# A delta-rule stage of a vision tower: the decay mask moved into spare rows of a product, the inverse rows reordered, the output product cut in two

## What is computed

```python
q = silu(x @ Wq);  k = l2norm(silu(x @ Wk));  v = silu(x @ Wv)
log_f = log_sigmoid(x @ Wf);  gamma = -sigmoid(x @ Wgamma)
gk = log_f[..., None]
a = k * gamma[..., None] * exp(gk)
def step(S, inp):                      # over the 38 tokens of an image
    Sp = S * exp(gkt)[..., None]
    u = einsum('bhk,bhkv->bhv', at, Sp) + vt
    S = Sp + einsum('bhk,bhv->bhkv', kt, u)
    o = einsum('bhk,bhkv->bhv', qt, S)
out = out * sigmoid(x @ Wg1 @ Wg2)     # then a layer norm and @ Wo
```

## Time and profile before

| | |
|---|---|
| Median of 3 executions | 1996.59 us (1990.41 to 1997.77) |
| The profiled execution: its time | 1989.77 us |
| Its span, first to last instruction | 1988.0 us |
| Mean granted TensorE clock | 0.857 of 2.4 GHz |
| Busy: PE, DVE, ACT, POOL | 1708.2, 1108.5, 656.6, 314.5 us |
| The 11 delta stages | 1303.05 to 1819.19 us of the span |
| A stage with all four parts (3 to 7) | 57.8 to 61.7 us |

### The profile page before, as it was taken

How to read it: one execution, slowest core, us unless ns; L and a number is a source line. 1 busy time by engine, 2 the same in 40 slices (tenths; PEclk the granted TensorE clock), 3 DMA queues, 4 the chain that set the end, 5 groups by cost and what they waited for, 6 DMA issues and landing times. The chain is left out here.

```text
span 1988.0 us, 51796 instructions
## 1 busy us (share of the span) xinstructions
PE 1708.2 (86%) x22689; PEld 1517.3 (76%) x22689; DVE 1108.5 (56%) x2379; ACT 656.6 (33%) x1347; POOL 314.5 (16%) x284
## 2 busy tenths in 40 slices
PE   4677786799999999999999999876888888757589
PEld 4466675579988999989999999745877777756468
DVE  3655555674545555455555465566445555543885
ACT  3334534433322233232223232163333333223142
POOL 0232232520000000000000000052322223200530
PEclk9888988899999999999999999877666656655579
DMA  4100000100100000000101000100000000001001
GB/s 135 60 2 1 0 0 1 67 22 1 43 1 22 22 22 22 22 22 1 44 1 43 1 1 1 36 1 2 4 4 4 3 4 4 4 4 48 1 11 41
DMA packets 10070, 36.01 MB, mean 18 GB/s; under 512 B 3056, under 2 KB 6152, under 8 KB 7304
## 3 DMA queue, kind: packets, MB, share of 16 engines
q1 hardware_dynamic: 9864, 32.96, 4.8%
HBM read 30.47 MB, written 2.49 MB: 17 GB/s over the span
## 5 line engine op out<-in xcount | busy, mean ns | idle before, releaser
L1042 ACT ACTIVATE hidden<-bank,moe_b 128x512 f32<-128x512 f32 (+1 forms) x320 | 213.3, 668 | 537.1 <-PE bank L934 524.5
L951 PE MATMUL bank<-moe_w2h,hidden_hi 128*128 128x256 f32 x1216 | 345.7, 284 | 0.0
L951 PE MATMUL bank<-moe_w2l,hidden_hi 128*128 128x256 f32 x1216 | 344.0, 283 | 0.0
L951 PE MATMUL bank<-moe_w2h,hidden_lo 128*128 128x256 f32 x1216 | 343.9, 283 | 0.0
L934 PE MATMUL bank<-x_hi,moe_w1h 128*128 128x512 f32 (+1 forms) x640 | 243.8, 381 | 2.9 <-ACT hidden L1042 2.8
L934 PE MATMUL bank<-x_lo,moe_w1h 128*128 128x512 f32 (+1 forms) x640 | 242.5, 379 | 0.0
L934 PE MATMUL bank<-x_hi,moe_w1l 128*128 128x512 f32 (+1 forms) x640 | 242.0, 378 | 0.0
L951 PEld LDWEIGHTS bank<-moe_w2h,hidden_hi 128*128 128x128 f32 x1216 | 233.1, 192 | 6.0 <-DVE residual L1076 4.3
L1076 DVE SCALAR_TENSOR_TENSOR residual<-bank,gates,residual 128x256 f32<-128x256 f32 x152 | 73.4, 484 | 290.4 <-PE bank L951 290.4
L951 PEld LDWEIGHTS bank<-moe_w2l,hidden_hi 128*128 128x128 f32 x1216 | 233.2, 192 | 1.2
L951 PEld LDWEIGHTS bank<-moe_w2h,hidden_lo 128*128 128x128 f32 x1216 | 233.2, 192 | 0.0
(11 more groups left out here) (287 smaller groups left out, 3357.3 us busy)
## 6 DMA issues: line engine op xcount, KB each, us to landing
moe_w<-in_moe_w SPq DMA_DIRECT2D x16, 1024.0 KB, 4.8
patches<-in_patches SPq DMA_DIRECT2D x8, 864.0 KB, 4.6
out<-residual SPq DMA_DIRECT2D x19, 128.0 KB, 1.7
ffn_w<-in_ffn_w SPq DMA_DIRECT2D x2, 1024.0 KB, 6.4
att_w<-in_att_w SPq DMA_DIRECT2D x1, 1536.0 KB, 5.9
delta_w<-in_delta_w SPq DMA_DIRECT2D x1, 1280.0 KB
tok_w<-in_tok_w SPq DMA_DIRECT2D x1, 768.0 KB, 4.1
delta_wvf<-in_delta_wvf SPq DMA_DIRECT2D x1, 272.0 KB
```

The lines of the kernel that those rows point to most:

```text
L951: mm = nc.tensor.matmul(bank[4 + n % 3][:, 0:D], left, right, start=(i == 0), stop=(i == len(passes) - 1))
L1042: nc.scalar.activation(H[:, i % 4, 0:n], bank[i % 4][:, 0:n], ACT.Relu, bias=b1[:, x, f:f + 1]).then_inc(acted, 1)
```

## The change

- The mask product L1506 goes, and with it `past`. Instead the free 13 rows of each group of 32 carry it: `here` has 0/1 values there, scaled by 2^30, and `after` has -1 there where it had 0, so that the two remaining products give a large negative sum where the mask was. For this ln2 loads more pieces (8 of `here` now from two sources, and 8 of `free_row`), and DVE has more small operations in stage 0.
- DVE's inverse rows go ahead: 6 to 12 before bounded(0), 13 between bounded(0) and bounded(1), 14 and 15 before the low parts, 16 before weigh(0), 17 before unit_key(0), 18 before weigh(4).
- `output` becomes output(0) (images 0 to 3, banks 2 and 3) and output(1) (banks 0 and 1), in the order key_norm(0), output(0), key_norm(1), output(1). output(0) waits for solution(0) alone. The copies follow in the same two parts, as many and as large as before.
- inverse_out(2) and inverse_back(2) stand ahead of decay(7).

```diff
-            blocks += [(slice(HB * r + HALF, HB * (r + 1)), slice(PAD * (r // 2) + SEQ, PAD * (r // 2) + SEQ + HB - HALF))
-                       for r in range(4)]
+            free = [(slice(HB * r + HALF, HB * (r + 1)), slice((HB - HALF) * r + 1, (HB - HALF) * (r + 1) + 1))
+                    for r in range(4)]
...
-                            + [(here[dst, :], ins["from_here"][src, :]) for dst, src in blocks],
+                            + [(here[dst, :], ins["from_here"][src, :]) for dst, src in blocks]
+                            + [(here[dst, :], ins["after"][src, 0:SEQ]) for dst, src in free]
+                            + [(free_row[dst, 0:2], ins["from_here"][SEQ:SEQ + HALF, SEQ - 2:SEQ])
+                               for dst, src in blocks]
+                            + [(free_row[dst, 0:2], ins["from_here"][0:HB - HALF, SEQ - 2:SEQ]) for dst, src in free],
...
-                nc.tensor.matmul(bank[4 + b % 2][:, 0:CT], identb[:, :], spread(past[:, :], 1, HPH),
-                                 start=True, stop=False)
                 for part in range(2):
                     mm = nc.tensor.matmul(bank[4 + b % 2][:, 0:CT], after[:, :],
                                           MS[:, b % 2, part].rearrange("p g t -> p (g t)"),
-                                          start=False, stop=(part == 1))
+                                          start=(part == 0), stop=(part == 1))
...
-                        pe.wait_ge(o_lo, 2)
+                        pe.wait_ge(o_lo, 4)
...
-            def output():
+            def output(j):
                 if y is None:
                     return
-                pe.wait_ge(u2_back, 4)
-                for p in range(IP):
+                pe.wait_ge(u2_back, 2 * (j + 1))
+                if j == 0 and c is not None:
+                    pe.wait_ge(v_out, 2)
+                for p in (2 * j, 2 * j + 1):
...
-                                    mm = nc.tensor.matmul(bank[s][32 * g:32 * g + 32, ts], UB[half(s), lane, :],
-                                                          pa_y[half(s), lane, 0, :], start=(e == 0), stop=(e == 1))
+                                    mm = nc.tensor.matmul(bank[2 - 2 * j + s][32 * g:32 * g + 32, ts],
+                                                          UB[half(s), lane, :], pa_y[half(s), lane, 0, :],
+                                                          start=(e == 0), stop=(e == 1))
...
             key_norm(0)
+            output(0)
             key_norm(1)
-            output()
+            output(1)
...
+            inverse_out(2)
             decay(7)
-            inverse_out(2)
             score(3)
...
             inverse_norms()
-            high_out(0)
-            high_out(1)
+            for j in range(2):
+                for s in range(2):
+                    high_out(j, s)
...
-                nc.vector.tensor_scalar(past[:, :], here[:, :], 1.0, -MASKED, ALU.subtract,
-                                        ALU.mult).then_inc(masks, 1)
+                nc.vector.tensor_scalar(free_row[:, 2:3], free_row[:, 0:1], -1.0, None, ALU.mult).then_inc(masks, 1)
+                nc.vector.tensor_scalar(free_row[:, 3:4], free_row[:, 0:1], PAST, 1.0, ALU.mult,
+                                        ALU.add).then_inc(masks, 1)
...
+                dve.wait_ge(masks, 1)
+                for s in range(2):
+                    nc.vector.tensor_scalar(
+                        after[half(s), half(1 - s)].rearrange("p (h s) -> p h s", h=2)[:, :, 0:HALF],
+                        here[half(s), :].rearrange("p (h s) -> p h s", h=2), 1.0, free_row[half(s), 2:3],
+                        ALU.subtract, ALU.mult).then_inc(masks, 1)
+                dve.wait_ge(masks, 6)
+                nc.vector.tensor_scalar(here[:, :], here[:, :], free_row[:, 3:4], None, ALU.mult).then_inc(masks, 1)
...
-            for t in range(6, 10):
+            for t in range(6, 13):
                 inverse_row(t)
             bounded(0)
+            inverse_row(13)
             bounded(1)
-            for t in range(10, 13):
-                inverse_row(t)
-            low_out(0)
-            low_out(1)
-            inverse_row(13)
             inverse_row(14)
+            inverse_row(15)
+            for j in range(2):
+                for s in range(2):
+                    low_out(j, s)
+            inverse_row(16)
             weigh(0)
             weigh(1)
-            inverse_row(15)
+            inverse_row(17)
             unit_key(0)
             unit_key(1)
-            inverse_row(16)
             weigh(2)
             weigh(3)
-            inverse_row(17)
             inverse_row(18)
             for b in range(4, CB):
                 weigh(b)
```

More of the change, by code:

```diff
@@ L53 @@
 MASKED = -1e30
+PAST = 2.0 ** 30
 @contextmanager
@@ L1413, in delta_stage @@
         "PA", "VH", "SH", "SL", "KQ", "SQ", "KX", "SV", "GZ", "LF", "RX", "PD", "LZ", "MS", "DS", "AS", "TT", "TS"))
-    (wh, wl, wvfh, wvfl, same, after, past, here, emask, ident, identb, XH, XL, xh_c, xl_c) = (buffers[n] for n in (
-        "wh", "wl", "wvfh", "wvfl", "same", "after", "past", "here", "emask", "ident", "identb", "XH", "XL",
-        "xh_c", "xl_c"))
+    (wh, wl, wvfh, wvfl, same, after, here, free_row, emask, ident, XH, XL, xh_c, xl_c) = (buffers[n] for n in (
+        "wh", "wl", "wvfh", "wvfl", "same", "after", "here", "free_row", "emask", "ident", "XH", "XL", "xh_c", "xl_c"))
     wgh, wgl, G1, wg2, wg2s = (buffers[n] for n in ("wgh", "wgl", "G1", "wg2", "wg2s"))
@@ L1809, in _ @@
             decay(6)
+            inverse_back(2)
             decay(7)
-            inverse_back(2)
         @block.vector
@@ L1910, in with_values, with low_out @@
                                         ALU.add).then_inc(rx_ready, 1)
-            def low_out(s):
+            def low_out(j, s):
                 if y is None:
                     return
-                dve.wait_ge(o_hi, 2 * (s + 1))
-                for m in range(HALVES):
-                    ts = xl_c[:, m, y].rearrange("p (i s t) -> p s i t", s=2, t=SEQ)[:, s]
-                    low = nc.vector.tensor_tensor(
-                        ts, bank[s][:, IP * m * SEQ:IP * (m + 1) * SEQ].rearrange("p (i t) -> p i t", t=SEQ),
-                        xh_c[:, m, y].rearrange("p (i s t) -> p s i t", s=2, t=SEQ)[:, s].bitcast(F32), ALU.subtract)
-                low.then_inc(o_lo, 1)
+                dve.wait_ge(o_hi, 2 * j + s + 1)
+                low, high = (t[:, :, y].rearrange("p m (i s t) -> p s m i t", s=2, t=SEQ)[:, s, :, 2 * j:2 * j + 2]
+                             for t in (xl_c, xh_c))
+                nc.vector.tensor_tensor(
+                    low, bank[2 - 2 * j + s][:, 0:4 * SEQ].rearrange("p (m i t) -> p m i t", m=HALVES, t=SEQ),
+                    high.bitcast(F32), ALU.subtract).then_inc(o_lo, 1)
             def gate_parts():
```

22 lines of the change are left out of this document (11 added, 11 removed).

## The result

The changed kernel takes 1975.72 us, the median of 6 executions (1970.33 to 1981.24), against 1995.76 for the kernel before on the same chip (1990.41 to 2002.16, 6 executions). The ratio is 0.9901, 95% interval 0.9882 to 0.9919: faster by 19.8 us, with bounds of 16 and 23.5. The forecast was 1973.0 with a range of 1963 to 1986.

A forecast was written before the change was run, and what follows sets the result against it. PE was taken to bound a full stage's first half, DVE the second. Gains of 27.15 us less losses of 3.55 gave 23.6: 1989.77 to 1966.2 profiled, plus 6.8 to a median of 1973, range 1963 to 1986.

The forecast's parts named there:

- DVE bounds the second half, and the rows are the gain: Full stages: PE binds the first half, DVE the second; rows 10 to 12 (2.65 us) move into DVE's early idle time.
- What binds next: After score(0), PE binds, 9.7 us to score(2); last weigh 4.7 us earlier, 3.0 with everything at 1.2 GHz; 3.9 taken.
- Score(0) 1.2 us earlier: Full stages: low parts end at 1551.3 instead of 1552.5, so score(0) starts 1.2 us earlier; otherwise the prediction is wrong.
- The other two signs: Prediction wrong if weigh(4) still waits for row 18 instead of score(2), or full stages' mean clock leaves 0.60 to 0.70.
- The output in halves: Output product: key_norm(1) between the halves fills part of the instruction supply stop, gaining about 1.0 us per full stage.
- The border's place: Removed mask products move the block border some 34 products on, to the middle of output(1); 0.5 to 1.2 us of stop left.
- The mask product: One product is 0.29 us at 1.2 GHz, about 0.15 at 2.4; 0.58 us ahead of key_norm(0), 0.3 in stage 1.
- Stages 8 to 10: Gains after the full stages: stage 8 about 2.4 us, stage 9 4.3, stage 10 0.65 from half the copies after the output.
- The loads: ln2: sixteen mask pieces instead of eight on SP's queue, 2.85 us lost, bounds 2.0 and 3.5.
- (a): Rival: two held multiplies of 1.0 us per full stage beside POOL's steps; stage gains 1.9, sum 13.6, 1983; chance 0.16.
- (b): Rival: the clock falls as PE loses its cheap wide work; 17.5 us lost, 6 left, 1990; chance 0.09.
- (c): Rival: output(0) stops at a block border, late bounded(1) holds DVE's rows, low parts and score(0); 10.4 us slower, 2007; chance 0.04.

The follow-up runs named there:

- e1: Kernel before with only DVE's inverse rows moved ahead (and inverse_out(2), inverse_back(2) ahead of decay(7)): 1973.70 us, ratio 0.9898.
- f3: Kernel before with inverse rows 10 to 15 ahead of the low parts, DVE's old order from there, inverse_out(2) behind decay(7): 1974.51 us, ratio 0.9904.
- e7: Kernel before with only inverse rows 10 to 12 moved ahead of bounded(0), the rest of DVE's order as before: 1994.89 us, ratio 1.0005.
- e4: Kernel before with inverse rows ahead and output in halves, the bf16 mask product kept: 1975.93 us, ratio 0.9901.
- e2: Kernel before with only the output and its copies in halves, key_norm(1) between the output halves: 1992.99 us, ratio 0.9991.
- e5: e4 with both key norms on PE ahead of both output halves: 1969.69 us, ratio 0.9888.
- f4: Kernel before with the rows ahead and 32 tiny products added at the end of PE's work in stage 0: 1974.35 us, ratio 0.9900.
- e3: Kernel before with only the mask part: no L1506 product, 8 more loads, more mask operations in stage 0: 1995.91 us, ratio 1.0017.
- f1: Kernel before with the rows ahead and the 8 mask loads on their own semaphore, waited for only by SP: 1973.31 us, ratio 0.9892.
- e8: Kernel before with the rows ahead and 64 tiny products added at the end of PE's work in stage 0: 1969.17 us, ratio 0.9884.
- e6: The whole change with its 16 mask loads on their own semaphore, waited for only by SP at the stage's end: 1967.55 us, ratio 0.9871.

## Why the prediction was right, and where its steps were not

The time came out 2.7 us above the forecast. What the sum said of the profile did not come out as well: it was to take 23.6 us off the profiled execution, to 1966.2, and the profiled execution after took 1976.24, 13.5 less. Of the largest term, 19.5 us for the five full stages, the traces show 12.5. I had added 6.8 us for the way from the profiled execution to the median, and the changed kernel's profiled execution lies at its median. That the forecast was nearly met owes as much to that, which is luck, as to the sum.

**DVE bounds the second half, and the rows are the gain: right.** e1 alone gives all of it, and f3 with e7 shows which rows. But I counted rows 10 to 12 as "2.65 us that now run in the idle time". e7 shows that they are worth nothing: behind bounded(1) DVE waited again for ACT, and the row I had shown for it has 2.04 us. What counts is what crosses the low parts, rows 13 to 15 with 3.74 us of work; my schedule happened to hold both, so its end time didn't suffer.

**What binds next: right, with the lower of the two bounds.** The timeline of stage 5 shows DVE waiting for score(2) ahead of weigh(4), as forecast. Counted from bounded(0), the last weigh was to end 20.8 us later (1544.8 to 1565.6) and ends 22.9 later. Score(0) is 0.75 us of that (forecast 6.65 after bounded(0), measured 7.40). Of the other 1.3 us PE has nearly all between score(0)'s start and score(2)'s end, 10.98 us for a forecast of 9.7. The four decays there take 2.89 us in place of 1.86, from their starts to those of the next instruction: three are at 1.2 GHz, where I had two, and each takes 0.80 there where I had put 0.58, by the mask product's wrong price (below). Inverse_out(0) takes 2.53 in place of 2.06; one of its product records starts 0.41 us after the one before, where its pairs of records start 0.11 apart, and it stands 126 records behind the output's restart at 1547.87. So this is most likely a supply stop again, one that the timeline merges into the row. The all-slow bound of 3.0 us per full stage was the better value than 3.9; measured are 2.5.

**Score(0) 1.2 us earlier: wrong.** This was one of my own signs that the prediction is wrong, and in stage 5 it is met: score(0) starts 40.02 us after the stage's start, against 39.99 before, and 0.13 us earlier on average. In e1, which has the whole gain, it even starts 0.9 us later (41.42). The 1.2 us were to come from the output in halves and from 0.58 us of mask products ahead of key_norm(0), and neither brought them; the head was 0.4 us longer and not 0.6 shorter. The gain came all the same: it lies in the tail, where fewer of DVE's rows stand ahead of the last weighs. The other two signs stayed away: weigh(4) waits for score(2), and the full stages' clock is 0.67 on average. Of what the profile was to show, the stops in the output average 1.17 us and not well under 1, score(0)'s wait for the low parts fell from 0.95 to 0.61 us on average and did not grow to 1.5, and the full stages average 56.5 us, above the 53.5 to 56 forecast.

**The output in halves: wrong.** I put 1.0 us per full stage on the shorter stop. The mechanism's first half holds: the stops in the output fall from 1.82 to some 1.17 us on average, and from 1.96 in e1 to 1.24 in e4. The second half doesn't: the time isn't won. Before and after, all issue stops of a full stage together are 3.06 us, but that equality is of several parts, since the rows alone raise them to 4.04 and the halves on top of the rows lower them to 3.28. In e2 the output saves 0.27 us of stops and all stops together grow by 0.54. Stage 4 of the changed kernel shows how a stop comes back:

```profile
1488.60 0.29 PE L1633 MATMUL bank<-qk_and_ak 64*32 64x38 f32 x12
1490.39 1.44 PE L1633 MATMUL bank<-qk_and_ak 64*32 64x38 f32 x116 [1.50 <-issue]
1491.76 0.87 PE L1511 MATMUL bank<-decay_steps,after 128*128 128x304 f32 x2
1492.88 0.53 PE L1534 MATMUL bank<-q_and_k,dk_in_pair 32*64 32x76 f32 x9 [0.25 <-DVE x_lo L1925]
1494.18 1.33 PE L1534 MATMUL bank<-q_and_k,dk_in_pair 32*64 32x76 f32 x55 [0.77 <-issue]
```

From the restart at 1490.39 come 116 products, two of the decay and 9 of score(0), 127 together, and PE stops again, until 3.79 us after that restart. Work that ends sooner only meets the next block's arrival sooner. That would be why e2 gains nothing and e5, with twice the stop in its output, loses nothing. For e4 it isn't enough: all its stops together are 0.76 us shorter than e1's, and its full stages are 0.3 us longer; where that time goes isn't shown. A second thing kept the halves from paying: ACT's norms stand in its queue ahead of the high parts and wait for bounded(1), so the first half's high parts start at 1547.70, 2.9 us after output(0) ended (1544.20 + 0.59). The Trainium skill ("Runtime: NRT & Kernel Launch", Instruction fetch mechanics) calls the crossing "mostly hidden"; that holds for the experts' wide products here, 5,628 records in 878 us without one issue stop, and not for runs of small ones, where e1 in stage 5 stops for 2.18 us and f4 for 2.56. What I had missed is that the supply has a rate and isn't a single delay: where two stops stand one block apart in these fourteen traces, restart to restart is 3.4 to 4.2 us, with a median of 3.75. Every issue stop of their delta stages stands a whole number of 128 records, short by 7 at most, behind the stop before it.

**The border's place: right in kind.** The mask products gone by a stage move its stops by their own number. e3, which changes nothing else there, has them after 190, 141, 220, 171 and 250, where 172, 243, 186, 129 and 200 were: 18, 26, 34, 42 and 50 records on, less a block of 128 in the second. The changed kernel is within two of that (190, 140, 93 and 219, 169, 122 and 248), and f4 moves them by 64. In stage 5 the two stops are 0.42 and 0.61.

**The mask product: mis-sized.** I divided a decay of three products by three. The rows don't allow it. Before, in stage 5, the two wide products start 0.04 us behind the mask product:

```profile
1554.39 0.43 PE L1506 MATMUL bank<-past,ident_bf 128*128 128x304 bf16 x1
1554.43 0.89 PE L1509 MATMUL bank<-decay_steps,after 128*128 128x304 f32 x2
```

From the decay's start to the next instruction it is 0.87 us with the mask product and 0.80 without (1551.37 to 1552.17 above); at 2.4 GHz 0.51 (decay(5), 1559.27 to 1559.78 before) and 0.48 (1559.67 to 1560.15 in the changed kernel). So a mask product is worth 0.03 to 0.07 us and not 0.15 to 0.29, all 64 at most 4.5 us; my terms of 0.58 per full stage and 0.3 in stage 1 should have been some 0.15 and 0.1 to 0.2. e3's full stages, 0.46 us shorter with eight of them gone, agree.

**Stages 8 to 10.** Stage 8 gave 2.4 as forecast. Stage 9 gave 2.5 in the changed kernel, against 4.3 forecast, but 3.9 in e1 and 4.8 in e4. PE at its end in the changed kernel, as the earlier trace rows:

```profile
1767.65 3.96 PE L1574 MATMUL bank<-ident,inverse 64*64 64x64 f32 x64
1773.33 0.94 PE L1574 MATMUL bank<-ident,inverse 64*64 64x64 f32 x12 [1.72 <-DVE inverse L1842]
```

The wait of 3.01 us is gone; inverse_out(2) still waits 1.72 for row 18, which I had forecast to vanish. The missing part lies in the stage's supply stops, 9.0 us before and 11.7 after, where e1 has 8.8 and e4 9.2. Stage 10 gained nothing: the copies behind the output did get 0.6 us shorter (2.36 to 1.77), and stops in front of them took that.

**The loads: mis-sized, 2.85 for 1.65.** The eight added issues took 2.82 us of SP's queue, as counted, but DVE starts 1.55 us after the last issue ends (1288.36 + 2.82 to 1292.73) where it took 2.71 before. The measured cost lies under my lower bound of 2.0 too. Stage 2 was 0.4 us shorter and not 0.5 longer; stages 0 and 1 were 0.65 and 0.76 longer (18.9 and 27.5). That can't be put on the mask part: stage 0 takes 19.5 to 19.6 us in e1, e2 and e4, which have none of it, and stage 1 takes 27.4 in f1, which hasn't either. What makes these two stages differ between executions stays open.

**The rivals.** (a) needs two held multiplies per stage ahead of what counts. There is one ahead of bounded(0), row 10's (1.06 us beside a POOL operation at 1538.14 that takes 1.21; its reduction of the same size takes 0.36), in time that was idle, and two behind the low parts, row 16's (1.39, where the larger row 17 takes 0.78) and, in part, row 18's (1.16, where its reduction takes 0.83). By size the traces are nearer to this rival than to the forecast, 2.5 us per full stage where it had 1.9 and the forecast 3.9, and 13.5 in all for its 13.6; but the held multiplies aren't the reason. (b): the clock of the full stages is 0.65 0.68 0.62 0.75 0.65, before 0.67 0.67 0.65 0.62 0.65; it didn't fall. But the rows alone had raised it: over whole executions the medians are 0.859 before, 0.868 to 0.872 in the six kernels that have the rows and neither the norm between the halves nor the mask part, 0.866 in e4 and 0.863 in the change. So something in the other two parts took a piece of the rise away, and that the mask product was cheap wide work may be a part of it; no run separates it. (c): output(0) does stop, in stages 5 and 7, and in stage 5 its mechanism shows on a small scale. The stop is 0.42 us, bounded(1) comes 3.50 us after bounded(0) where 2.6 was forecast, and DVE reaches the low parts late: ACT's last high part is done at 1549.09, the last low part only at 1549.89, some 0.5 us later than it could be.

**What stays open.** The heads differ by up to 1.2 us between kernels whose first half is the same (e4 and e5). The issue stops in the head go the same way, 1.61 us in e4 and 1.06 in e5, and 0.91 before against 1.61 in e1, which is about half of the first difference and nearly all of the second. No run separates cause from chance here.

## What to carry to other kernels

Before you move work into an engine's idle time, follow the engine to its next wait: if it waits again before the work's old place, the two gaps are one, and only work that crosses the second one counts. Divide a group of pipelined products by its count only if the rows show where the next instruction starts with and without one of them. A stop that is due to a rate, as instruction supply is in long runs of small products, isn't surely won back by filling it: count all the stops of the stage, in every variant, and not the one that you aim at. And when an edit takes waits out, look at the granted clock behind it: here it rose with the rows, and a part of the gain may be its.

## What the runs showed of the hardware

- Product records that run at 0.012 us each outrun the supply: every 128 records PE can stop, for up to 2.6 us here, and from one such restart to the next it is 3.4 to 4.2 us. A product on fp32 data counts as two records (64 products of 32x32 by 32x16 stand as 128, e8).
- Shorter waits in a stage went with longer supply stops: 3.8 to 4.0 us per full stage in the kernels with the rows alone, 3.0 to 3.1 before and in e7.
- PE's waits for DVE in the tail fell from 2.6 to 0.35 us in e1, and the granted clock there rose from 0.69 to 0.84.
- A bf16 product ahead of two fp32r products with their own weights added only 0.03 to 0.07 us to the three.
- Small loads took 0.35 us each to issue on SP's queue, and a wait for the last of sixteen held DVE for 2.44 us; in e6, where DVE waits only for what it reads, it doesn't stop there.
